# One block for the down stage and the state-space stage, a reordered first normalisation, and query and key parts stored in stacked form

## The chip, the cores and the metric

The kernel runs on one core of one Trainium2 chip. The metric is the device time of one execution in microseconds (us). A core has TensorE (PE, with its weight loads as PEld), VectorE (DVE), ScalarE (ACT), GpSimd (POOL) and SyncE (SP), which here issues every transfer; sixteen DMA engines carry the transfers out. Each engine runs its own list of instructions in order, and they meet in semaphores.

## The reference, cut to what matters

```python
x = L0_attn_x                                   # 2 batches, 512 tokens, 512 features, float32
xn = layernorm(x)
x = x + attention(xn) + ffn(xn)                 # 32 heads of 16; 512 -> 1376 -> 512
xn = layernorm(x)
x = x + state_space(xn) + lora_ffn(xn)          # in_proj 512 -> 18560, conv of 4, scan in chunks

# state_space: proj = xn @ in_proj_w.T, split into gate, xBC and dt (128 heads)
dt  = softplus(dt + dt_bias)
cum = cumsum(dt * A)                            # within a chunk
dlast, cdec = exp(cum[-1] - cum), exp(cum[-1])  # decays, per head and chunk
```

All is float32. The kernel multiplies in three products of a high and a low half (`product`: low by high, high by low, high by high), so each 512-column product of depth 512 is 12 matmuls.

## The kernel before

There are four blocks (a block ends when all engines have met): QKV with the first normalisation, attention with the gate and up products, down with the second normalisation, and the state-space stage with the output. The state-space stage takes the time from 514 us on and is touched at its beginning alone. Tokens are 8 tiles of 128 (`NTOK`); a batch is four of them.

**First normalisation** (`FirstNorm`). For each tile: DVE `moments` (L242, L244), ACT `root` (L217), DVE `scalars` (L248, L250), ACT `normalise` (L222), PE `turn` (four transposes, L210), ACT `high` (L227), DVE `low` (L255). ACT's loop does, for step t, `root(t)`, `normalise(t - 1)`, `high(t - 2)`; DVE's does `moments(t)`, `scalars(t - 1)`, `low(t - 2)`. PE does turns 0 to 4, 12 matmuls of `half(0, 0)`, turns 5 and 6, `half(1, 0)`, turn 7, and then `half(0, 1)`, which waits for the last `low`.

**QKV.** Twelve weight tiles pass through four slots (`Feed`: SP `load` L129, ACT `split_hi` L137, DVE `split_lo` L148). Tiles 0 to 7 give query and key rows: ACT `hi` (L503) and DVE `lo` (L522) make their halves, and SP's `parts(n)` stores the halves to DRAM (`qk_parts`, L427), 512 KB each. Tiles 8 to 11 are the value weights; the first value product needs all four, tile by tile. SP's order is written out: `load(n)`, then `parts(n - 6)`, and for parts 1 to 3 a `stack`, which loads the halves back with the partitions arranged as hi, hi, lo for queries and hi, lo, hi for keys (L329). Before the first `stack` SP waits until the parts of tiles 0 and 1 have landed. On ACT `split_hi(n)` stands ahead of `hi(n - 4)`. After the value product of token tile t PE does two `row_step`s (L341), the first of which waits for all eight `lo`.

**Down stage** (`emit_down`). PE adds the products of down and output projection into eight PSUM banks, one a token tile (12 matmuls each for the last four steps). DVE `add(t)` forms x and its moments, ACT takes the root, DVE `scale(t)` normalises, PE `turn_norm(t)` (L877) transposes into the same bank, ACT and DVE `low(t)` (L994) make xhi and xlo, PE `turn_sum(t)` (L883) transposes the sum into the bank again, ACT copies it and SP stores it. DVE's `low(t - 1)` comes between `add(t)` and `scale(t)`.

**Beginning of the state-space stage** (`emit_ssm`). PE multiplies the dt tile (24 matmuls into banks 2 and 3), then the entries of `ENTRIES`: B, C, g0, x0, x1, g1, x2, ... of 24 matmuls each, alternately in banks 0, 1 and 2, 3. Before entry e PE waits until entry e - 2 has been read: for B, C and x by DVE's `conv` (L1668), which needs ACT's `first_tap` (L1510). From dt come a chain of ACT and DVE work (`DT_SUM`: the cumulative sums, L1751 to L1766), then the exponentials on ACT (`DT_EXP`: L1594 and L1596), and after entries 4 and 5 PE transposes cum, dt and decays in six groups (L1468), which DVE copies out (L1773); the fifth group waits for the first copy. SP's written order around this is:

```python
            for e in range(rank(FIRST, is_tile) + AHEAD + 2):
                if e >= feed.begun:
                    weight((0, e))
                if e == 5:
                    sp.wait_ge(dt_dve, 5 + NTOK)
                    sp.dma_start(c.cum_dram[:, 0].rearrange("n h t -> h n t"), cum).then_inc(cum_out, 16)
                    sp.wait_ge(dt_act, 5 + NTOK)
                    sp.dma_start(c.cum_dram[:, 1].rearrange("n h t -> h n t"), ecum).then_inc(cum_out, 16)
                    with nc.allow_non_contiguous_dma("one value per head and chunk"):
                        sp.dma_start(c.dec_dram, ecum[:, :, CS - 1]).then_inc(cum_out, 16)
```

so weight 6 is issued behind the store of the chunk decays (`dec_dram`, called chunk_decays in the profile: 1,024 values of 4 bytes). On ACT the split of weight e + 2 of the ranked tiles, `high`, stands ahead of the tap of entry e.

Of the kernel before, what the change touches and what calls it, by code (L numbers as in the profile page):

```python
# [19 lines left out]
P = 128  # L20
# [140 lines left out]
class FirstNorm:  # L161
# [133 lines left out]
class Stacks:  # L295
# [23 lines left out]
    def stack(self, sp, c, it, i):  # L319
# [3 lines left out]
        r = it * P + i // 2 * 64  # L323
        for row, dst, side, part in ((0, self.qs, 0, 0), (1, self.qs, 0, 0), (2, self.qs, 0, 1),
                                     (0, self.ks, 1, 0), (1, self.ks, 1, 1), (2, self.ks, 1, 0)):
            for half in range(2):
                src = c.qk_rows[part, side, bass.ds(r + half * 2 * DK, 2 * DK), i % 2 * L:(i % 2 + 1) * L]
                at = half * HALF + row * DK
                sp.dma_start(dst[at:at + DK, i, :, :].bitcast(F32),  # L329
                             src.rearrange("(h d) t -> d h t", h=2)).then_inc(self.stacked[i], 16)  # L330

    def row_step(self, pe, rows, it, i, u, deep):

        n = it * NB + i
        if u == 0:
            pe.wait_ge(self.stacked[i], (it + 1) * 12 * 16)
# [57 lines left out]
def emit_qkv(nc, c, w, x_load, xhi, xlo, st, feed, tile_done, next_feed):  # L394
# [3 lines left out]
    with ExitStack() as ctx:  # L398
# [24 lines left out]
        def _(sp):  # L423
            def parts(n):
                sp.wait_ge(qk_l, n + 1)
                for part, src in enumerate((qk_hi, qk_lo)):
                    sp.dma_start(c.qk_dram[part, n % 2 * KT + n // 2], src[:, n % NR, :].bitcast(F32)  # L427
                                 ).then_inc(parts_out[n % NR], 16)
                if n == 1:
                    for s in parts_out[0:2]:  # L430
                        sp.wait_ge(s, 32)
# [16 lines left out]
            for i, s in enumerate(parts_out):  # L448
                sp.wait_ge(s, len(range(i, nqk, NR)) * 32)
# [49 lines left out]
        def _(act):  # L499
            def hi(n):  # L500
                act.wait_ge(tile_done, n + 1)
                after(act, parts_out[n % NR], n // NR * 32)
# [297 lines left out]
def emit_down(nc, c, w, xhi, xlo, hid, feed, tile_done, att_moved, oe, dt_feed, ssm_feed):  # L800

    with ExitStack() as ctx:
        sem = lambda n: ctx.enter_context(nc.semaphore(f"down_{n}"))
# [21 lines left out]
        block = ctx.enter_context(nc.Block())  # L825
# [5 lines left out]
        @block.sync  # L831
        def _(sp):
# [26 lines left out]
            for s in x_out:  # L859
                sp.wait_ge(s, NTOK // 2 * 16)  # L860

        @block.tensor
        def _(pe):
# [22 lines left out]
            for t in range(NTOK):  # L886
# [16 lines left out]
        @block.scalar  # L903
        def _(act):
# [26 lines left out]
            for t in range(NTOK + 2):  # L931
                if 1 <= t <= NTOK:
                    act.wait_ge(turned, t)
                    act.activation(xhi[:, :, tokens(t - 1)], turned_tile(t - 1), ACT.Copy).then_inc(hi_done, 1)
# [4 lines left out]
                if t >= 2:  # L939
                    act.wait_ge(x_turned, t - 1)  # L940
                    after(act, x_out[t % 2], (t - 2) // 2 * 16)
                    act.activation(xt[:, t % 2, :, :], turned_tile(t - 2), ACT.Copy).then_inc(x_copied, 1)

        @block.vector
        def _(dve):
# [58 lines left out]
        @block.gpsimd  # L1004
        def _(pool):
# [9 lines left out]


def emit_ssm(nc, c, w, xhi, xlo, feed, tile_done, dt_feed, dt_tile, semaphores, x_out):
# [14 lines left out]
    with ExitStack() as ctx:  # L1032
# [63 lines left out]
        DT_SUM, DT_EXP, DT_TURN = 1, 2, 4  # L1096
# [155 lines left out]
        def _(sp):  # L1252
# [970 lines left out]
```

## Time and profile before

| | |
|---|---|
| median of 3 runs | 2131.8 us (2131.57 to 2133.14) |
| the profiled execution, its own time | 2133.82 us |
| span of its profile | 2132.1 us, mean granted clock 0.992 |
| PE busy | 2081.6 us, 98% of the span |
| DVE, ACT, POOL busy | 69%, 63%, 41% |
| DMA | 305.34 MB, 143 GB/s on average |

Times in the profile count from the start of the span. A row of a timeline gives start and duration in us, the engine, the line, the operation with output and inputs, how many were merged, and in brackets how long the engine sat idle before it and what released it. Matmuls are pipelined, so that one of 0.39 us is followed by the next after 0.23 us; the distance of starts tells the pace.

### The profile page before, as it was taken

To read this page: it belongs to the slowest core of one execution; us is meant where nothing else is said; L and a number is where in the kernel's file an instruction comes from. 1 tells how busy PE (TensorE), PEld (TensorE's weight loads), DVE (VectorE), ACT (ScalarE), POOL (GpSimd) and SP (SyncE) were. 2 spreads that over 40 slices of the span, in tenths; PEclk is the share of its full clock that TensorE was granted. 3 is DMA by queue.
4 is the path that set the end of the run, shared out by engine and by line. 5 is a ranking of instruction groups with operands and counts; after the bars stand their busy time and mean duration, and the time that the engine had idled before them with its cause. 6 is when DMAs were issued, how large, how long until landed. Compare 5 with 4: busy or idle time off the path is not lost.

```text
span 2132.1 us, 33690 instructions
## 1 busy us (share of the span) xinstructions
PE 2081.6 (98%) x12040; PEld 1550.1 (73%) x12040; DVE 1462.3 (69%) x1811; ACT 1337.6 (63%) x2376; POOL 869.6 (41%) x762
## 2 busy tenths in 40 slices
PE   7899999998999999999999999999999999999999
PEld 5644444486777777777777777777777767888887
DVE  4466666285578778778878788687787775555555
ACT  4255555543587877888878787887878783333322
POOL 1011110130157666666757667675766682000000
PEclk9999999999999999999999999999999999999999
DMA  4422222241545555545545545555455467444452
GB/s 158 158 81 74 73 79 62 70 151 55 124 139 166 167 152 163 165 144 171 156 153 171 161 149 161 158 164 161 155 159 167 149 190 257 153 148 148 144 183 89
DMA packets 182781, 305.34 MB, mean 143 GB/s; under 512 B 20416, under 2 KB 96704, under 8 KB 182496
## 3 DMA queue, kind: packets, MB, share of 16 engines
q1 hardware_dynamic: 182624, 303.29, 45.8%
q8 instruction: 94, 1.54, 0.3%
q14 instruction: 63, 0.52, 0.1%
HBM read 249.90 MB, written 53.06 MB: 142 GB/s over the span
## 4 chain that ended last, share of the span: by engine, by line
PE 71%; ACT 2%; DVE 1%; POOL 1%; issue 1%; DMA 1%; DVEq 0%; SPq 0%; POOLq 0%; ACTq 0%
PE ssm_pp L156 16%; PE ssm_pp L158 15%; PE ssm_pp L157 15%; PE ssm_py L1444 5%; PE ssm_py L1439 4%; PE ssm_pstate L1423 4%; PE ssm_turn L1400 2%; PE ssm_py L158 1%; PE ssm_py L157 1%; PE ssm_py L156 1%; PE ssm_pp L1383 1%; PE ssm_pstate L158 1%; PE ssm_pstate L157 1%; PE ssm_pstate L156 1%; PE ssm_turn L158 1%; PE ssm_turn L157 1%
## 5 line engine op out<-in xcount | busy, mean ns | idle before, releaser
L156 PE MATMUL ssm_pp<-xhi,ssm_lo 128*128 128x512 f32 x1192 | 479.4, 402 | 4.2 <-DVE ssm_bc L1668 3.5
L158 PE MATMUL ssm_pp<-xhi,ssm_hi 128*128 128x512 f32 x1192 | 466.0, 391 | 0.0
L157 PE MATMUL ssm_pp<-xlo,ssm_hi 128*128 128x512 f32 x1192 | 465.7, 391 | 0.0
L1556 ACT ACTIVATE ssm_sct<-ssm_cumb,ssm_gpar 128x128 f32<-128x128 f32 x1024 | 313.1, 390 | 72.0 <-DMA ssm_cumb<-dt_sums 48.7
L148 POOL TENSOR_TENSOR ssm_lo<-ssm_raw,ssm_hi 128x512 fp32r<-128x512 f32 x150 | 244.1, 1633 | 92.5 <-ACT ssm_hi L137 92.5
L156 PEld LDWEIGHTS ssm_pp<-xhi,ssm_lo 128*128 128x128 f32 x1192 | 224.0, 188 | 67.5 <-issue 18.7
L1668 DVE SCALAR_TENSOR_TENSOR ssm_xc<-ssm_pp,vectors,ssm_xc 128x1022 f32<-128x1022 f32 (+2 forms) x192 | 245.2, 1277 | 36.2 <-ACT ssm_xc L1510 31.5
L158 PEld LDWEIGHTS ssm_pp<-xhi,ssm_hi 128*128 128x128 f32 x1192 | 224.2, 188 | 48.2
L157 PEld LDWEIGHTS ssm_pp<-xlo,ssm_hi 128*128 128x128 f32 x1192 | 224.3, 188 | 42.7
L1703 DVE TENSOR_TENSOR ssm_sct<-ssm_sct,ssm_cbm 128x1024 f32<-128x1024 f32 x128 | 228.4, 1785 | 27.7 <-ACT ssm_sct L1563 27.7
L1845 POOL TENSOR_TENSOR ssm_go<-ssm_t,ssm_gt 128x512 f32<-128x512 f32 x128 | 165.0, 1289 | 172.1 <-DVE ssm_t L1739 172.1
L767 ACT ACTIVATE att_pt<-att_keys 128x512 f32<-128x512 f32 x256 | 143.9, 594 | 136.0 <-PE att_keys L657 135.8
L2035 ACT ACTIVATE xlo<-ssm_gt 128x1024 fp32r<-128x1024 f32 x64 | 67.8, 1060 | 238.9 <-PE ssm_turn L158 228.1
L351 DVE TENSOR_REDUCE stk_mx<-att_rows 128x2 f32<-128x1024 f32 x112 | 137.3, 1226 | 90.5 <-PE att_rows L341 90.5
L148 POOL TENSOR_TENSOR ffn_lo<-ffn_raw,ffn_hi 128x512 fp32r<-128x512 f32 x33 | 42.9, 1301 | 375.8 <-ACT ffn_hi L137 375.8
L1715 DVE TENSOR_TENSOR ssm_xp<-ssm_turn,ssm_gpar 128x512 f32<-128x512 f32 x128 | 87.8, 686 | 151.2 <-PE ssm_turn L1400 151.2
L1444 PE MATMUL ssm_py<-ssm_sct,ssm_xp 128*64 128x128 f32 x2048 | 184.3, 274 | 0.0
L2072 DVE TENSOR_TENSOR xlo<-ssm_gt,xlo 128x1024 fp32r<-128x1024 f32 x64 | 78.4, 1225 | 149.2 <-ACT xlo L2035 149.2
L1822 POOL TENSOR_TENSOR ssm_xw<-ssm_xp,ssm_gpar 128x512 f32<-128x512 f32 x96 | 127.2, 1325 | 110.3 <-DVE ssm_xp L1715 110.2
L1439 PE MATMUL ssm_py<-ssm_cecl,ssm_state 128*64 128x128 f32 x1536 | 154.1, 279 | 0.1
L1739 DVE SCALAR_TENSOR_TENSOR ssm_t<-ssm_xc,vectors,ssm_py 128x128 f32<-128x128 f32 x512 | 142.4, 336 | 5.3 <-PE ssm_py L1444 5.3
L1444 PEld LDWEIGHTS ssm_py<-ssm_sct,ssm_xp 128*64 128x64 f32 x2048 | 124.5, 137 | 24.3 <-DVE ssm_xp L1715 18.2
(287 smaller groups left out, 4151.4 us busy)
## 6 DMA issues: line engine op xcount, KB each, us to landing
ssm_cumb<-dt_sums SPq DMA_DIRECT2D x96, 1024.0 KB, 5.9
ssm_raw<-w SPq DMA_DIRECT2D x150, 256.0 KB, 5.6
gated<-ssm_go SPq DMA_DIRECT2D x128, 256.0 KB, 4.3
ssm_cumb<-dt_sums SPq DMA_DIRECT2D x32, 512.0 KB, 4.0
ssm_gt<-w SPq DMA_DIRECT2D x64, 256.0 KB, 2.7
ssm_xc<-gated SPq DMA_DIRECT2D x32, 512.0 KB, 4.2
ssm_sct<-gated SPq DMA_DIRECT2D x32, 512.0 KB, 4.3
ffn_raw<-w SPq DMA_DIRECT2D x37, 256.0 KB, 2.8
```

Source lines behind the costliest of these rows:

```text
L148: i = dve.tensor_tensor(lo, src, hi, ALU.subtract)
L156: pe.matmul(out, wlo, xhi, start=start, stop=False)
L157: pe.matmul(out, whi, xlo, start=False, stop=False)
L158: return pe.matmul(out, whi, xhi, start=False, stop=stop)
L767: act.activation(pt[:, kt % 2, PAIRED[u % HQ], :], keys[:, u % 2, :], ACT.Exp).then_inc(exp_done, 1)
L1439: pe.matmul(p_y[r * HP:(r + 1) * HP, s % 2, ct, :], state[:, ch % 2, h * HP:(h + 1) * HP], cecl[:, s % 2, h, :], start=True, stop=False)
L1444: mm = pe.matmul(p_y[r * HP:(r + 1) * HP, s % 2, ct, :], xp[:, s % 2, h * HP:(h + 1) * HP], sct[:, s % 2, h, :], start=(ch == 0), stop=True)
L1556: i = act.activation(sct[:, s % 2, h, :], cumb[:, s % 2, 0, h, :], ACT.Relu, scale=-1.0, bias=gpar[:, unit, 0, s % NTOK, h:h + 1])
L1668: i = dve.scalar_tensor_tensor(dst[:, :, sh:L], pp[:, e % 2, :, 0:L - sh], col(conv_col(g, e) + tap), dst[:, :, sh:L], ALU.mult, ALU.add)
L1703: dve.tensor_tensor(sct[:, s % 2, :, :], sct[:, s % 2, :, :], cbm[:, s % NTOK, :].unsqueeze(1).broadcast_to([P, HU, CS]), ALU.mult).then_i ...
L1739: i = dve.scalar_tensor_tensor(t2[:, s % 2, ct, :], xc[:, s // NTOK, ct, t * CS:(t + 1) * CS], col(g * (2 * CU) + (V_D + s // NTOK * CU + ...
L1845: pool.tensor_tensor(go[:, s % 2, :, :], t2[:, s % 2, :, :], gt[:, s // NTOK, :, t * CS:(t + 1) * CS], ALU.mult).then_inc(g_done, 1)
```

## The change

1. **First normalisation:** on ACT `high(t - 2)` moves ahead of `root(t)` and `normalise(t - 1)`.
2. **Query and key parts:** DRAM now holds, for each tile, 8 heads by 3 rows (hi, hi, lo or hi, lo, hi) by 16 by tokens. `parts(n)` makes three stores of 512 KB instead of two, and `stack` makes four loads of 48 partitions instead of twelve of 16.
3. **One block:** the down stage's parts become functions of an object that the state-space block calls first, so no meeting of the engines lies between. The turns of the down stage run one tile later, and between the last turns PE does the first batch's half of the dt tile and of the B tile. B's first tap moves ahead of the logarithm on ACT, and `DT_SUM` and `DT_EXP` move one entry later, the exponentials behind the tap of x0.

```diff
     def scalar(self, act, feed):
         for t in range(NTOK + 2):
+            if t >= 2:
+                self.high(act, t - 2)
             if t < NTOK:
                 self.root(act, t)
             if 1 <= t <= NTOK:
                 self.normalise(act, t - 1)
-            if t >= 2:
-                self.high(act, t - 2)
...
-        r = it * P + i // 2 * 64
-        for row, dst, side, part in ((0, self.qs, 0, 0), (1, self.qs, 0, 0), (2, self.qs, 0, 1),
-                                     (0, self.ks, 1, 0), (1, self.ks, 1, 1), (2, self.ks, 1, 0)):
+        for side, dst in enumerate((self.qs, self.ks)):
             for half in range(2):
...
-                sp.dma_start(dst[at:at + DK, i, :, :].bitcast(F32),
-                             src.rearrange("(h d) t -> d h t", h=2)).then_inc(self.stacked[i], 16)
+                src = c.qk_heads[side, bass.ds(it * (P // DK) + (i // 2 * HQ + half * 2), 2), :,
+                                 i % 2 * L:(i % 2 + 1) * L]
+                at = half * HALF
+                sp.dma_start(dst[at:at + KSTACK, i, :, :].bitcast(F32),
+                             src.rearrange("h q t -> q h t")).then_inc(self.stacked[i], 16)
...
-                for part, src in enumerate((qk_hi, qk_lo)):
-                    sp.dma_start(c.qk_dram[part, n % 2 * KT + n // 2], src[:, n % NR, :].bitcast(F32)
+                for row, src in enumerate((qk_hi, qk_hi, qk_lo) if n % 2 == 0 else (qk_hi, qk_lo, qk_hi)):
+                    sp.dma_start(c.qk_dram[n % 2 * KT + n // 2, :, row, :, :], src[:, n % NR, :].bitcast(F32)
                                  ).then_inc(parts_out[n % NR], 16)
...
-    c.qk_dram = scratch("qk_parts", (2, 2 * KT, P, T))
-    c.qk_rows = c.qk_dram.rearrange("a (s n) p t -> a s (n p) t", s=2)
+    c.qk_dram = scratch("qk_parts", (2 * KT, P // DK, 3, DK, T))
+    c.qk_heads = c.qk_dram.rearrange("(s n) h r d t -> s (n h) (r d) t", s=2)
...
                 mm.then_inc(summed, 1)
-                if t >= 1:
-                    turn_norm(t - 1)
                 if t >= 2:
-                    turn_sum(t - 2)
+                    turn_norm(t - 2)
+                if t >= 3:
+                    turn_sum(t - 3)
+            turn_norm(NTOK - 2)
+            turn_sum(NTOK - 3)
+            dt_tile(pe, 0)
+            turn_norm(NTOK - 1)
             turn_sum(NTOK - 2)
-            turn_norm(NTOK - 1)
+            first_tile(pe, 0)
             turn_sum(NTOK - 1)
...
             for t in range(NTOK):
                 add(t)
-                if t >= 1:
-                    low(t - 1)
+                if t >= 2:
+                    low(t - 2)
                 scale(t)
+            low(NTOK - 2)
             low(NTOK - 1)
...
-        DT_SUM, DT_EXP, DT_TURN = 1, 2, 4
+        DT_SUM, DT_EXP, DT_TURN = 2, 3, 4
...
+            down.sync(sp)
             for e in range(rank(FIRST, is_tile) + AHEAD + 2):
                 if e >= feed.begun:
                     weight((0, e))
                 if e == 5:
+                    down.sums_written(sp)
                     sp.wait_ge(dt_dve, 5 + NTOK)
...
+            down.tensor(pe, dt_product, first_tile)
+            down.all_tokens(pe)
+            dt_product(pe, 1)
+            first_tile(pe, 1)
+            for e in range(1, FIRST):
...
             act.activation(dt, e_, ACT.Exp, scale=-1.0).then_inc(dt_act, 1)
+            first_tap(0, 0)
             act.wait_ge(dt_act, 3)
             act.activation(da, dt, ACT.Ln, bias=c.ones[:, 0:1]).then_inc(dt_act, 1)
             for e in range(FIRST):
-                if e == DT_EXP:
...
                     if rank(e, is_tile) + AHEAD >= feed.begun:
                         high((0, rank(e, is_tile) + AHEAD))
-                    if is_conv(e):
+                    if is_gate(e):
+                        silu(0, e)
+                    elif e > 0:
                         first_tap(0, e)
-                    else:
-                        silu(0, e)
+                    if e == DT_EXP:
+                        act.wait_ge(dt_dve, 5 + NTOK)
+                        for t in range(NTOK):
+                            act.activation(dl[:, t, :], cum[:, t, :], ACT.Exp, scale=-1.0,
+                                           bias=cum[:, t, CS - 1:CS]).then_inc(dt_act, 1)
+                        act.activation(ecum, cum, ACT.Exp).then_inc(dt_act, 1)
```

## Rows read from the trace of the kernel before

**Rows 1.** The page: busy time of each engine.

```profile
PE 2081.6 (98%) x12040; PEld 1550.1 (73%) x12040; DVE 1462.3 (69%) x1811; ACT 1337.6 (63%) x2376; POOL 869.6 (41%) x762
```

**Rows 2.** Timeline of ScalarE in the first normalisation.

```profile
7.66 0.81 ACT L222 ACTIVATE stk_v<-stk_v,ln_shift,ln_rstd 128x512 f32<-128x512 f32 x1
8.67 0.60 ACT L227 ACTIVATE xhi<-qkv_pv 128x512 fp32r<-128x512 f32 x1 [0.21 <-PE qkv_pv L210]
...
20.63 0.81 ACT L222 ACTIVATE stk_v<-stk_v,ln_shift,ln_rstd 128x512 f32<-128x512 f32 x1
...
23.86 0.81 ACT L222 ACTIVATE stk_v<-stk_v,ln_shift,ln_rstd 128x512 f32<-128x512 f32 x1
```

**Rows 3.** Timeline of TensorE in the first normalisation.

```profile
18.28 1.11 PE L210 MATMUL qkv_pv<-ident,stk_v 128*128 128x128 f32 x4 [2.10 <-ACT stk_v L222]
19.48 0.79 PE L156 MATMUL qkv_ps<-xhi,qkv_lo 128*128 128x512 f32 x1
...
24.72 0.66 PE L210 MATMUL qkv_ps<-ident,stk_v 128*128 128x128 f32 x4
...
29.96 0.50 PE L156 MATMUL qkv_ps<-xhi,qkv_lo 128*128 128x512 f32 x1 [1.41 <-DVE xlo L255]
```

**Rows 4.** Timeline of SyncE, which issues the transfers, in QKV.

```profile
36.29 0.43 SPq L427 DMA_DIRECT2D qk_parts<-qk_lo  x1
...
43.65 2.67 SPq L329 DMA_DIRECT2D stk_qs<-qk_parts  x6
...
68.29 1.01 SPq L129 DMA_DIRECT2D qkv_raw<-w  x1
...
96.19 1.55 SPq L382 DMA_DIRECT2D stk_qs<-stk_nmh  x2
```

**Rows 5.** Timeline of TensorE where QKV turns to the value product.

```profile
74.61 0.79 PE L156 MATMUL qkv_pv<-qkv_hi,xlo 128*128 128x512 f32 x1 [2.12 <-DVE qkv_lo L148]
...
76.19 1.22 PE L341 MATMUL qkv_ps<-stk_ks,stk_qs 48*128 48x512 f32 x4
...
82.20 0.73 PE L341 MATMUL qkv_ps<-stk_ks,stk_qs 48*128 48x512 f32 x4
```

**Rows 6.** Timeline of ScalarE: the last value weights' split.

```profile
73.21 0.63 ACT L137 ACTIVATE qkv_hi<-qkv_raw 128x512 fp32r<-128x512 f32 x1 [1.56 <-DMA qkv_raw<-w]
```

**Rows 7.** Windows: length, five engines' busy time, granted clock, DMA share, GB/s.

```profile
70.00:73.00 3.00, 0.98 (x3) 0.48 (x3) 1.92 (x2) 1.54 (x2) 0.00 (x0) 1.00 1.03 412
```

**Rows 8.** DMA issues of the run: count, KB each, us to landing.

```profile
qk_parts<-qk_hi SPq DMA_DIRECT2D x8, 512.0 KB, 3.9
...
stk_qs<-stk_nmh SPq DMA_DIRECT2D x32, 4.0 KB
...
chunk_decays<-ssm_xc SPq DMA_DIRECT2D x1, 4.0 KB, 10.1
```

**Rows 9.** Timeline of TensorE from the down stage's end to x0.

```profile
482.71 0.66 PE L877 MATMUL down_ps<-ident,ffn_h 128*128 128x128 f32 x4 [1.19 <-DVE ffn_h L989]
...
504.06 0.60 PE L877 MATMUL down_ps<-ident,ffn_h 128*128 128x128 f32 x4
...
514.10 0.77 PE L156 MATMUL ssm_pp<-xhi,dtw_lo 128*128 128x512 f32 x1 [3.74 <-PEq L802]
...
527.12 0.39 PE L156 MATMUL ssm_pp<-xhi,ssm_lo 128*128 128x512 f32 x1
...
542.05 0.62 PE L156 MATMUL ssm_pp<-xhi,ssm_lo 128*128 128x512 f32 x1 [3.50 <-DVE ssm_bc L1668]
```

**Rows 10.** Timeline of ScalarE: the last exponential, the split of weight 6.

```profile
540.52 1.04 ACT L1596 ACTIVATE ssm_xc<-ssm_gt 128x1024 f32<-128x1024 f32 x1
...
552.32 0.63 ACT L137 ACTIVATE ssm_hi<-ssm_raw 128x512 fp32r<-128x512 f32 x1 [1.76 <-DMA ssm_raw<-w]
```

**Rows 11.** Timeline of VectorE: a convolution and the first copies.

```profile
556.03 3.91 DVE L1668 SCALAR_TENSOR_TENSOR ssm_xc<-ssm_pp,vectors,ssm_xc 128x1022 f32<-128x1022 f32 x3 [1.53 <-ACT ssm_xc L1510]
559.86 0.87 DVE L1773 COPY ssm_gt<-ssm_py 128x128 f32<-128x128 f32 x4
```

More of the change, by code:

```diff
@@ L930, in _, with high, copy_sum @@
             ssm_feed.begin_hi(act)
[L931 to L934, printed above, removed]
+            def high(t):
+                act.wait_ge(turned, t + 1)
+                act.activation(xhi[:, :, tokens(t)], turned_tile(t), ACT.Copy).then_inc(hi_done, 1)
+            def copy_sum(t):
+                act.wait_ge(x_turned, t + 1)
+                after(act, x_out[t % 2], t // 2 * 16)
+                act.activation(xt[:, t % 2, :, :], turned_tile(t), ACT.Copy).then_inc(x_copied, 1)
+            for t in range(NTOK + 3):
+                if 2 <= t < NTOK + 2:
+                    high(t - 2)
                 if t < NTOK:
@@ L938, in _, with vector @@
                                    ).then_inc(std_done, 1)
[L939 to L945, printed above, removed]
+                if t >= 3:
+                    copy_sum(t - 3)
+        def vector(dve):
             def invert(k, half):
@@ L1014, in _, with sums_written, emit_ssm @@
             ssm_feed.begin_lo(pool)
-def emit_ssm(nc, c, w, xhi, xlo, feed, tile_done, dt_feed, dt_tile, semaphores, x_out):
+        self.sync, self.tensor, self.scalar, self.vector, self.gpsimd = sync, tensor, scalar, vector, gpsimd
+        self.first_tokens = lambda pe: pe.wait_ge(lo_done, NTOK // B)
+        self.all_tokens = lambda pe: pe.wait_ge(lo_done, NTOK)
+        self.bank_free = lambda pe, bank: pe.wait_ge(x_copied, bank + 1)
+        def sums_written(eng):
+            for q in x_out:
+                eng.wait_ge(q, NTOK // 2 * 16)
+        self.sums_written = sums_written
+def emit_ssm(nc, c, w, xhi, xlo, feed, tile_done, dt_feed, dt_tile, semaphores, down, x_out):
     with ExitStack() as ctx:
@@ L1446, in scan, with dt_product @@
                 mm.then_inc(y_done, 1)
-            pe.wait_ge(dt_feed.lo_done, 1)
-            for b in range(B):
+            def dt_product(pe, b):
+                down.bank_free(pe, B + b)
+                if b == 0:
+                    pe.wait_ge(dt_feed.lo_done, 1)
+                    down.first_tokens(pe)
                 for k in range(KT):
@@ L1453, in _, with first_tile @@
                                  xlo[:, k, b * L:(b + 1) * L], k == 0, k == KT - 1)
-            mm.then_inc(dt_tile, 1)
-            for e in range(FIRST):
+                if b == B - 1:
+                    mm.then_inc(dt_tile, 1)
+            def first_tile(pe, b):
+                down.bank_free(pe, b)
+                entry(0, 0, range(b, b + 1))
+            down.tensor(pe, dt_product, first_tile)
[3 more added lines that the diff above has]
+            for e in range(1, FIRST):
                 if e == 1:
@@ L1590, in _ @@
             for e in range(FIRST):
-                if e == DT_EXP:
-                    act.wait_ge(dt_dve, 5 + NTOK)
-                    for t in range(NTOK):
-                        act.activation(dl[:, t, :], cum[:, t, :], ACT.Exp, scale=-1.0,
-                                       bias=cum[:, t, CS - 1:CS]).then_inc(dt_act, 1)
-                    act.activation(ecum, cum, ACT.Exp).then_inc(dt_act, 1)
                 if ENTRIES[e] == "turn B":
@@ L1860, in low @@
                 feed.split_lo(pool, gg * GT, rr)
+            down.gpsimd(pool)
             for s in marks.cleared:
```

46 lines of the change are left out of this document (19 added, 27 removed).

## The prediction

> **What bounds the kernel now.** The page says that TensorE is busy 98% of the span [rows 1]. Busy time of pipelined matmuls hides their pace, so I read TensorE's timeline for the places where it stands still or runs at its lower clock, and then the other engines' timelines around those places. Everywhere else I take TensorE as the bound, and what other engines gain there is worth nothing. The change touches three such places: TensorE's starts in the first normalisation [rows 3], the two waits for value weights at 71.5 and 74.6 us, the second of 2.12 us [rows 5], and the seam from the down stage to the state-space stage, where TensorE starts the dt tile at 514.10 after 3.74 idle and waits again, 3.50, at 542.05 [rows 9]. In attention, waits for a transfer never stop TensorE, so fewer stack loads there are worth nothing: the work that hides them is the products of gate and up.
>
> **First normalisation.** No instruction is added; two pieces of ScalarE's order swap. Before, normalise(1) ran at 7.66, ahead of high(0), which could start only at 8.67, when TensorE had turned tile 0 [rows 2]. Now it stands behind high(0) and a root: 8.67 plus 0.5 plus 0.24, so about 9.4, 1.75 us late. Before, normalise(5) to normalise(6) was 3.2 us (20.63 to 23.86) [rows 2], and so were the tiles before. The new cycle is normalise 0.8, turn 1.1 [rows 3], high 0.6 and root 0.25, so 2.75. Tiles 2 to 5 then start at 12.1, 14.9, 17.6 and 20.4: tile 4's turn comes at 18.4 instead of 18.28, and the first product again at about 19.4 [rows 3]. Up to there nothing is won. After it things get worse: TensorE has 12 matmuls (19.48 to 24.18) before turn 5, high(5) waits for that turn, and normalise(6) now stands behind high(5). It starts at 24.7 plus 0.5 plus 0.25, so 25.4 instead of 23.86 [rows 2]. Turn 6, at 24.72 before [rows 3], waits until 26.3; half(1, 0) takes 2.8, turn 7, high and low 2.0 more, and the product of the second batch starts at 31.5 instead of 29.96. Cost **+1.6**; bounds 0 (if high(5) were never late) and +2.4 (if the lost time also lowers the clock for a while).
>
> **Parts and stacks.** SyncE's issue of six loads takes 2.67 us or more [rows 4]. Eight fewer loads per stack save some 3.6 us of SyncE each time, for three stacks; that is the delay which makes the last value weights late: issued at 68.29 [rows 4], split at 73.21 [rows 6], needed by TensorE at 70.2 if nothing stalled. Against it stand one more store of 512 KB per tile, which adds half to the stored bytes, and the form of all three. Before, a store's destination is 128 rows. Now it is 8 heads, each a run of 16 rows, with gaps between heads, so its outermost count is 8. If a transfer is dealt to engines along that count, 8 of 16 carry it. The nearest transfers of such a form here are the copies of negated maxima, of 8 runs: each takes SyncE 0.65 to 0.78 (1.55 for two) where a store of 128 rows takes 0.43 [rows 4], and the list of issues gives them no time to landing although it gives one for the stores [rows 8]. So something in their completion differs; they are too small to show a rate. With the engines all at work the trace shows a DMA share of 1.03 at 412 GB/s [rows 7], so the engines themselves are full, and eight of them would carry about 208 GB/s.
>
> This place the Trainium skill speaks to. "DMA: Bandwidth & Descriptors", section "Why a DMA increments its semaphore by 16 and not by 1", states that the engines used are the largest number up to 16 that divides both patterns' slowest dimension; by it the new stores would run on 8 engines and the sum would be that of eight engines below. No row here shows the rate of such a store.
>
> *With eight engines.* A store takes 524 KB / 208 = 2.5 us on the low eight, three take 7.5, and tiles come every 5.4 (24 matmuls of 0.227). A stack's loads, now of 48 rows, take all engines, 786 KB at about 310 GB/s, 2.5; a weight tile 0.65. The engines start 0.8 after the first issue, at 36.7. Parts 0, weight 7 and parts 1 end at 52.4; SyncE, which waits for them (it went on at 43.65 before [rows 4]), goes on at 53.1. The queue then holds in order stack, weight 8, parts 2, stack, weight 9, parts 3, stack, weight 10, parts 4, weight 11: three times 2.5, four times 0.65, three times 7.5, so 32.6 us, plus 0.8 until the first load moves, from 53.1: 86.5, and with landing about 87.4. Before, the split began at 73.21 [rows 6], so weights 11 come 14.2 late. Rows step 0 followed the split by 2.98 (76.19) [rows 5]; the same follows now, lower clock included. The remaining three tiles of stores end near 110, before TensorE's last row step near 118. Cost **+14.2**.
>
> *With sixteen engines.* The engines have 3.4 MB until the first wait ends (45.6) and 8.1 MB more, at 415 GB/s and 310 for stacks: weights 11 land near 67 to 69, in time. The first row steps come at 71.0, and the lower clock between 76.19 and 82.20 (6.0 us for a step that takes 3.6 at full clock) is gone: row step 1 at 74.6 instead of 82.20 [rows 5]. Gain **-7.6**.
>
> I take eight engines: of the two nearest kinds, the copies of 8 runs share the form, and the 128-row stores don't.
>
> **The seam.** Before the loop's end TensorE no longer waits for x at 482.71 (1.2, with the slow pick-up 1.35), and two turns move behind it, 0.9: the last product ends at 501.75 instead of 504.06 [rows 9]. Then come four turns, of which turn_sum(5) waits for low(5), now behind add(7), until 504.2; dt's first half 2.8 and two turns, B's first half and one turn, then dt's and B's second halves: C starts at 517.0. Before it started at 527.12 [rows 9]. So the seam itself gives 10.1. What of it survives? On VectorE and ScalarE follow z, Abs, Exp, B's tap at 517.9, B's convolution 519.05 to 522.95, C's to 527.7, the sums to 533.1; x0's product ends at 534.1, its tap at 535.3; then the table load 1.3 and the exponentials 3.4, which end at 540.0. Before they ended at 541.56 (540.52 plus 1.04) [rows 10]. Only 1.5 us is left, because the exponentials now wait for x0's tap. Behind them SyncE stores the decays, which need 10.1 us to land [rows 8], and weight 6 is queued behind: split at 552.32 before [rows 10], 550.8 now. Behind that split on ScalarE stands x1's tap, then x1's convolution 3.9 on VectorE, then the first copy 0.87 [rows 11]; TensorE's fifth group of transposes, which was at 562.07, waits for that copy: 557.2. TensorE has finished g1 at 546.6 and idles 10.5 us, loses 1.9 to the lower clock afterwards (as after 542.05, nine matmuls at 0.43 instead of 0.23), and ends x2 at 565.9 instead of 568.4. Gain **-2.6**. Bounds: -11 if the decays' store were no obstacle, 0 if weight 6 lands 2.6 later. Semaphores, buffers and the stores of x cost nothing: SyncE issues weights 3 to 5 at 512.7, before 514.06.
>
> **The sum.** +14.2 + 1.6 - 2.6 = **+13.2**. The profiled execution took 2133.82 (span 2132.1), 2.0 over the median of the runs; I put the difference on the median: 2131.8 + 13.2 = **2145.0**.
>
> **Rivals.** A measurement here can tell about 0.2%, 4.3 us, from no change.
>
> *All sixteen engines carry the stores.* The other side: -7.6 + 1.6 - 2.6 = -8.6, 2123.2, and down to 2115 with a full seam. For it: every large transfer in the trace fills all engines [rows 7]. It decides at the rate at which these stores run: at 208 GB/s they cost 14.2; the sum is zero where weights 11 land 1 us after the old time, at about 300 GB/s; above it the change wins. Chance 0.18. The Trainium skill's same page, section "Specifications", gives about 358 GB/s as a core's share of HBM; the trace shows 412 in a stretch of stores [rows 7], and by 358 this rival would gain some 3 us less.
>
> *The seam keeps its gain.* The decays' slow store doesn't hold weight 6 back, for instance because it overlaps with other traffic less than before; -11 instead of -2.6, with eight engines 2136.6. Against it: the 10.1 us stand for a transfer of 4 KB, so not its bytes but its form is slow. Chance 0.12.
>
> *Eight engines, each faster than its share.* If 412 GB/s is a limit of something shared, eight could carry 300: three stores 5.2, weights 11 at 75.8, +2.6 + 1.6 - 2.6: 2133.4. Against it: DMA share 1.03, engines full. Chance 0.08.
>
> The forecast has what is left, 0.62, with its own range 2139 to 2150 (first normalisation 0 to 2.4, issue and landing of each store +-0.2, ten of them before weights 11, +-2).
>
> **How the numbers follow.** Slower by over 0.2%: 0.62 + 0.12 + 0.02 = 0.76. Within: 0.05. Faster: 0.19. The range that leaves out 2 in 10 at most reaches from the sixteen-engine case, 2121, to 2150.
>
> **What would show it.** Right: stores of parts with a duration over 0.6 on SyncE and a DMA share near 0.5 with about 208 GB/s where only they run; last qkv split near 89 (the 1.6 included); the first row step near 92; batch two's first product at 31.5; TensorE idle for some 10 us before the fifth group of transposes. Wrong: stores at 400 GB/s, or value weights split before 75; exponentials that end more than 4 us earlier against the last down product.

## The result, and the profile after

The changed kernel takes 2152.15 us (median of 4 runs, 2151.57 to 2154.48) where the kernel before took 2132.47 in the same session: ratio 1.0090, 95% interval 1.0077 to 1.0103, **19.7 us slower**. Forecast was 13.2 us slower, 2145.0 with a range of 2139 to 2150: the direction held and the size did not. The profiled execution took 2152.64 (span 2150.9, mean granted clock 0.988).

TensorE's timeline after the change, the places that answer to [rows 3, 5, 9]:

```profile
31.71 0.50 PE L156 MATMUL qkv_ps<-xhi,qkv_lo 128*128 128x512 f32 x1 [1.41 <-DVE xlo L255]
69.73 0.76 PE L156 MATMUL qkv_ps<-xhi,qkv_lo 128*128 128x512 f32 x1 [5.08 <-DVE qk_lo L521]
89.71 0.80 PE L156 MATMUL qkv_pv<-qkv_hi,xlo 128*128 128x512 f32 x1 [8.99 <-DVE qkv_lo L148]
97.73 0.80 PE L156 MATMUL qkv_pv<-qkv_hi,xlo 128*128 128x512 f32 x1 [6.37 <-DVE qkv_lo L148]
99.31 1.22 PE L340 MATMUL qkv_ps<-stk_ks,stk_qs 48*128 48x512 f32 x4
104.47 0.73 PE L340 MATMUL qkv_ps<-stk_ks,stk_qs 48*128 48x512 f32 x4
...
546.29 0.50 PE L156 MATMUL ssm_pp<-xhi,ssm_lo 128*128 128x512 f32 x1 [0.35 <-DVE ssm_bc L1696]
579.09 1.09 PE L1494 MATMUL ssm_py<-ident,ssm_xc 128*128 128x128 f32 x4 [8.98 <-DVE ssm_gt L1802]
```

The reader is to see three things. The second batch starts at 31.71 and not at 29.96. Then TensorE stands still four times for weights or for halves that stand behind a weight's split (the three long waits are shown, the fourth is 0.92 at 79.75); the first row step comes at 99.31 and not at 76.19 [rows 5], the second at 104.47 and not at 82.20. And at the seam the wait of 3.50 for B's convolution is 0.35 now, while a new one of 8.98 stands before the fifth group of transposes.

SyncE's timeline, which answers to [rows 4]:

```profile
37.66 1.47 SPq L426 DMA_DIRECT2D qk_parts<-qk_hi  x2
39.17 2.65 SPq L426 DMA_DIRECT2D qk_parts<-qk_lo  x1
41.86 1.79 SPq L129 DMA_DIRECT2D qkv_raw<-w  x1
43.70 1.52 SPq L426 DMA_DIRECT2D qk_parts<-qk_hi  x1
45.27 1.95 SPq L426 DMA_DIRECT2D qk_parts<-qk_lo  x1
47.26 1.46 SPq L426 DMA_DIRECT2D qk_parts<-qk_hi  x1
59.70 0.81 SPq L328 DMA_DIRECT2D stk_qs<-qk_parts  x2
```

SyncE has issued its sixth store by 48.7 and goes on at 59.70; before, it went on at 43.65 [rows 4]. What the engines did in that time and after it, in windows of 4 us, columns as in [rows 7] (the last three are TensorE's granted clock, the DMA share, which is the mean busy share of the sixteen DMA engines, and GB/s):

```profile
40.00:44.00 4.00, 4.00 (x19) 3.33 (x18) 0.70 (x2) 1.01 (x2) 0.00 (x0) 1.00 0.50 124
48.00:52.00 4.00, 4.00 (x19) 3.32 (x18) 0.00 (x0) 0.00 (x0) 0.00 (x0) 1.00 0.51 179
52.00:56.00 4.00, 4.00 (x19) 3.31 (x18) 1.92 (x2) 1.55 (x2) 0.00 (x0) 1.00 0.51 211
60.00:64.00 4.00, 4.00 (x19) 3.34 (x18) 0.00 (x0) 0.00 (x0) 0.00 (x0) 1.00 0.86 170
92.00:96.00 4.00, 0.00 (x0) 0.00 (x0) 0.00 (x0) 0.00 (x0) 0.00 (x0) 0.50 0.51 206
```

Where stores fill the queue (52 to 56, 92 to 96) the share is 0.51 and the rate 206 to 211. The trace's records of single packets say the same: at most moments of these windows 8 packets are under way at once, and from 70 to 73 us in the kernel before there are 16. So half of the engines work, each as fast as before. But from 40 to 44 the stores run at 124 with the same share, and the stack's loads (60 to 64) at 170 with a share of 0.86.

ScalarE's splits of the weights behind parts and stacks; the last answers to [rows 6]:

```profile
66.79 0.63 ACT L137 ACTIVATE qkv_hi<-qkv_raw 128x512 fp32r<-128x512 f32 x1 [13.14 <-DMA qkv_raw<-w]
...
96.32 0.63 ACT L137 ACTIVATE qkv_hi<-qkv_raw 128x512 fp32r<-128x512 f32 x1 [6.48 <-DMA qkv_raw<-w]
```

A table of five places in the profiled executions (us) says where time went or came from. "Copy of B" is ScalarE's copy of B by token, behind the whole seam; from it to the end of the span it is 1550.8 before and 1550.0 after.

| | second batch | attention's first product | down's first product | copy of B | down to copy |
|---|---|---|---|---|---|
| before | 29.96 | 107.53 | 415.06 | 581.28 | 166.2 |
| changed | 31.71 | 129.75 | 438.37 | 600.89 | 162.5 |
| difference | +1.75 | +22.2 | +23.3 | +19.6 | -3.7 |

By place that is 1.75 up to the second batch, 20.5 from there to attention, 1.1 within attention (307.5 became 308.6; experiments 1 and 6, both with the old parts, show 307.3 and 308.6, so this is scatter), -3.7 at the seam, and -0.8 behind it: 18.8, the difference of the spans. These are single executions. The seam of before, unchanged in five of the experiments below (3 to 7), takes 164.6 to 165.4 there and 166.2 here; with the one block it takes 161.5 to 163.2 in three executions (the changed kernel, experiments 1 and 2). By the medians, 165.4 and 162.5, the seam gives 2.9 and not 3.7. Attention's start scatters too: four executions with the QKV block of before have it at 106.8 to 108.1.

### The profile page after: what moved, and what is told of

Its sections match the earlier page's. It is cut to its first block, busy times and chain, and to the rows that moved or that the text cites. A ratio compares the mean times of both kernels' runs of the same rounds, so it can differ in the third digit from the quotient of the medians.

```text
span 2150.9 us, 33464 instructions
## 1 busy us (share of the span) xinstructions
PE 2082.9 (97%) x12040; PEld 1551.1 (72%) x12040; DVE 1466.9 (68%) x1811; ACT 1336.5 (62%) x2376; POOL 870.4 (40%) x762
## 4 chain that ended last, share of the span: by engine, by line
PE 74%; ACT 2%; DVE 1%; POOL 1%; DMA 1%; issue 1%; SPq 0%; DVEq 0%; POOLq 0%; ACTq 0%
PE ssm_pp L156 16%; PE ssm_pp L158 15%; PE ssm_pp L157 15%; PE ssm_py L1457 5%; PE ssm_py L1452 4%; PE ssm_pstate L1436 4%; PE ssm_turn L1413 2%; PE ssm_py L156 1%; PE ssm_py L157 1%; PE ssm_py L158 1%; PE down_ps L156 1%; PE down_ps L158 1%; PE down_ps L157 1%; PE ssm_pp L1396 1%; PE ssm_pstate L158 1%; PE ssm_pstate L157 1%
```

## The experiments

Each was timed in five rounds beside the kernel before. The ratios are to it, with 95% intervals.

**1. Old parts put back.** The changed kernel with the removed lines of `stack` and `parts` (two stores, twelve loads) again.

> The changed kernel with the old parts and stacks (two stores, twelve loads) put back; the reordered first normalisation and the one block stay. Theory: the whole loss lies in the parts and stacks. The trace of the changed kernel shows its attention block 22.2 us later than before, 1.75 of it from the first normalisation, and the seam gives 3.7 back; so 2132.5 + 1.75 - 3.7 = about 2130.5, a little faster than before. Rival: the loss lies in the first normalisation or in the long block (another arrangement of memory, other waits); then this kernel stays above 2137.

2130.78, ratio 0.9990 (0.9981 to 0.9999). All of the loss was in parts and stacks. The seam, from down's first product to the copy of B, takes 163.2: 3.0 less than the 166.2 of the kernel before, 2.2 less than the median with the old seam.

**2. Three stores to 128 rows.**

```diff
-                    sp.dma_start(c.qk_dram[n % 2 * KT + n // 2, :, row, :, :], src[:, n % NR, :].bitcast(F32)
+                    sp.dma_start(c.qk_dram[n % 2 * KT + n // 2, :, row, :], src[:, n % NR, :].bitcast(F32)
...
-    c.qk_dram = scratch("qk_parts", (2 * KT, P // DK, 3, DK, T))
-    c.qk_heads = c.qk_dram.rearrange("(s n) h r d t -> s (n h) (r d) t", s=2)
+    c.qk_dram = scratch("qk_parts", (2 * KT, P, 3, T))
+    c.qk_heads = c.qk_dram.rearrange("(s n) (h d) r t -> s (n h) (d r) t", s=2, d=DK)
```

> The changed kernel with the same three stores of 512 KB and four loads a stack, but with the three rows of each partition side by side in DRAM, so that a store goes to 128 rows one behind the other and not to 8 heads of 16. Bytes and number of stores are those of the changed kernel. Theory of the form (eight engines): the DMA share passes 0.9 while stores run, and the time comes down to 2123 by the prediction's sum, or, with the stacks' loads at the 180 to 200 GB/s which the changed kernel's trace shows for them and not at 310, to about 2131. Rival, bytes: one more store a tile and more SyncE work cost what was lost; then the time stays within 3 us of 2152.

2131.65, ratio 0.9991 (0.9982 to 1.0000), 20.5 us less than the changed kernel by the medians of two sessions, with its bytes, stores and loads. Windows of this kernel, columns as above:

```profile
48.00:52.00 4.00, 4.00 (x19) 3.31 (x18) 1.91 (x2) 1.28 (x2) 0.00 (x0) 1.00 0.93 192
52.00:56.00 4.00, 4.00 (x19) 3.33 (x18) 0.83 (x2) 1.55 (x2) 0.00 (x0) 1.00 1.04 366
72.00:76.00 4.00, 0.64 (x4) 0.20 (x2) 1.65 (x2) 1.51 (x2) 0.00 (x0) 0.75 1.04 422
```

Where stores fill the queue (72 to 76) they run at 422 with a share of 1.04. The stack's loads (48 to 52) move 192 GB/s and still take 0.93 of the engines. It isn't faster than experiment 1, though: from 52 to 84 us the share is 1.02 to 1.05, where in experiment 1 it falls to 0.51 to 0.56 between stacks (56 to 60, 64 to 68). My reading is that the third store fills the time that the eight saved loads had freed.

**3. New parts alone**, in the kernel before.

> The kernel before with nothing but the new parts and stacks. If the three parts of the change add up, this shows the parts' term by itself: predicted +14.2, and by the trace of the changed kernel +20.5 (22.2 less 1.75), so 2153 and not 2146.7. Rival: the term is 14.2 and the other 6 us come from the late start that the reordered normalisation gives the transfers.

2152.86, ratio 1.0089 (1.0076 to 1.0103). Attention starts at 128.68, +21.2. The terms add up: 21.2 here against 22.2 in the changed kernel, and the late start of the normalisation isn't what made the term large.

**4. The form alone.** Two stores and twelve loads as before, with a gap behind every head (the loads read from the new places).

```diff
-                    sp.dma_start(c.qk_dram[part, n % 2 * KT + n // 2], src[:, n % NR, :].bitcast(F32)
+                    sp.dma_start(c.qk_dram[part, n % 2 * KT + n // 2, :, 0:DK, :], src[:, n % NR, :].bitcast(F32)
...
-    c.qk_dram = scratch("qk_parts", (2, 2 * KT, P, T))
+    c.qk_dram = scratch("qk_parts", (2, 2 * KT, P // DK, DK + 1, T))
```

> The kernel before, its two stores and twelve loads, with one change: in DRAM each head of 16 rows is followed by an empty row, so that a store goes to 8 runs of 16 rows. Bytes, stores and loads stay as they were. Theory of the form: stores at about half rate, DMA share near 0.5 where only they run; the wait of SyncE for the first four stores ends about 8 us later, the last value weights come some 11 us later, so 2143 (2140 to 2147). Rival, bytes: no change, 2132.5.

2150.36, ratio 1.0082 (1.0068 to 1.0096): 17.6 us, nearly the whole of experiment 3 and more than my 11. Attention starts 20.2 late, against 21.2 there: the form costs 20, and the third store with the larger loads about 1, which is within the scatter of that start. My 11 counted the stores and left out that SyncE is held up behind them. The first wait ends at 52.77, 9.1 late. The first group of six loads then takes 2.67, as before [rows 4], but the second takes 7.93 (4.14 before) and the third 7.29 (5.05 before), and from the end of that wait to the last split it takes 12.5 longer than before:

```profile
60.03 7.93 SPq L329 DMA_DIRECT2D stk_qs<-qk_parts  x6
72.56 7.29 SPq L329 DMA_DIRECT2D stk_qs<-qk_parts  x6
```

Its windows:

```profile
36.00:40.00 4.00, 4.00 (x19) 3.34 (x18) 1.92 (x2) 1.31 (x2) 0.00 (x0) 1.00 0.34 63
44.00:48.00 4.00, 4.00 (x20) 3.30 (x19) 0.00 (x1) 0.32 (x1) 0.00 (x0) 1.00 0.50 189
92.00:96.00 4.00, 0.00 (x0) 0.00 (x0) 0.51 (x1) 1.17 (x2) 0.00 (x0) 0.50 0.51 204
```

**5. Four runs instead of eight** (the same with `(2, 2 * KT, 4, 2 * DK + 1, T)` and stores to `0:2 * DK`).

> The kernel before, its two stores and twelve loads, with an empty row in DRAM behind every 32 rows, so that a store goes to 4 runs of 32 rows and not to 8 of 16. Theory that a store is dealt to as many engines as its destination has runs: 4 engines, a DMA share near 0.25 and about 103 GB/s where only stores run, a store of 512 KB takes 5.1 us; SyncE's first wait ends near 62 and the last value weights are split at 103 to 110, so 2132 + 30 to 38, 2162 to 2170. Rival: any gap in the destination halves the rate (longer runs do no harm or help a little); then 2150 or less, as with 8 runs, with a share of 0.5.

2176.69, ratio 1.0200 (1.0186 to 1.0214). SyncE goes on at 62.04 as expected; the last split is at 110.70, 0.7 past the late end of what I gave, and the time is 7 us above my range. The value products of a later tile also wait (5.27 at 143.24, for a copy of ScalarE), which my sum didn't have. The windows show the number of engines:

```profile
48.00:52.00 4.00, 4.00 (x19) 3.33 (x18) 0.00 (x0) 0.00 (x0) 0.00 (x0) 1.00 0.25 103
108.00:112.00 4.00, 0.00 (x0) 0.00 (x0) 0.64 (x1) 1.30 (x2) 0.00 (x0) 0.50 0.26 105
```

Four runs: share 0.25, 103 to 105 GB/s. Eight: 0.51, 204 to 211. 128 rows: 1.04, 422. By the packet records 4, 8 and 16 packets are under way at once, and a packet of 4,096 bytes takes 0.159 us in each of the three. Longer runs are slower, so the gap isn't the cost; the number of runs is. This is what the Trainium skill's "DMA: Bandwidth & Descriptors" says in "Why a DMA increments its semaphore by 16 and not by 1": the engines used are the largest number up to 16 that divides the slowest dimension of both patterns. The traces agree with it at 4, at 8 and at 128. They can't tell it from the plainer rule "as many engines as runs, at most 16"; a count such as 12 or 20, where the two could part, wasn't tried.

**6. The first normalisation alone.**

> The kernel before with nothing but the reordered first normalisation. Predicted +1.6; the trace of the changed kernel shows the second batch's first product 1.75 later, so 2134.3 if all of it reaches the end. Rival: the kernel with old parts and new normalisation shows that start at 31.18 and its attention block only 0.8 later than before, because the wait for the last value weight is set by transfers and takes up a part; then 2132.5 to 2133.5.

2132.92, ratio 1.0008 (0.9999 to 1.0017). The second batch starts at 30.98, +1.0, and attention at 107.66, +0.1. The rival is closer: the wait for the last value weights takes up nearly all of it, though the start of attention scatters by more than the difference. With the interval from 0 to 3.6 us the time can't tell the two.

**7. The parts in pairs**, a version that keeps the bytes of before and all sixteen engines.

```diff
-                for part, src in enumerate((qk_hi, qk_lo)):
-                    sp.dma_start(c.qk_dram[part, n % 2 * KT + n // 2], src[:, n % NR, :].bitcast(F32)
+                for row, src in enumerate((qk_hi, qk_lo) if n % 2 == 0 else (qk_lo, qk_hi)):
+                    sp.dma_start(c.qk_dram[n % 2 * KT + n // 2, :, row, :], src[:, n % NR, :].bitcast(F32)
...
+                sp.dma_start(dst[at:at + 2 * DK, i, :, :].bitcast(F32),
+                             heads.rearrange("h d r t -> (d r) h t")).then_inc(self.stacked[i], 16)
+                sp.dma_start(dst[at + 2 * DK:at + 3 * DK, i, :, :].bitcast(F32),
+                             heads[:, :, side, :].rearrange("h d t -> d h t")).then_inc(self.stacked[i], 16)
```

> The kernel before with another layout of the parts: high and low row of a partition side by side (low and high for keys), two stores a tile to 128 rows, and a stack of eight loads (four of 32 partitions, four of 16) and not twelve. Bytes as before. If SyncE's issue of loads is what makes the last value weights late (wait of 2.12 us and a lower clock behind it), this gives 3 to 6 us: 2127 to 2129. Rival: the transfers themselves, loads of stacks at 180 to 200 GB/s, set the time; then within 1.5 us of 2132.5.

2126.99, ratio 0.9978 (0.9969 to 0.9987), 4.7 us faster. Its timeline of TensorE:

```profile
73.19 0.50 PE L156 MATMUL qkv_pv<-qkv_hi,xlo 128*128 128x512 f32 x1 [2.41 <-DVE qkv_lo L148]
74.63 0.73 PE L342 MATMUL qkv_ps<-stk_ks,stk_qs 48*128 48x512 f32 x4 [0.48 <-DVE qk_lo L523]
78.28 0.73 PE L342 MATMUL qkv_ps<-stk_ks,stk_qs 48*128 48x512 f32 x4
```

A wait of 2.41 and a short one of 0.48 are left of the two, and from the first row step to the second it is 3.65 and not 6.01 [rows 5]: the granted clock is 1.00 from 72 to 80 here and falls to 0.50 there. The last split comes at 71.78, only 1.4 earlier than before, so 2.4 of the gain is the clock in this execution. The same QKV code ran once more with the lower clock (experiment 9). The time lies in the range of my theory, but the rival held in part: the last value weight is issued at 62.44, 5.9 earlier than before [rows 4], and its split gains only those 1.4, after 2.81 of waiting for the transfer. The engines were full meanwhile (from 60 to 68 us a share of 1.03 to 1.06 at 253 to 272 GB/s), so the transfers, and no longer SyncE's issue, set that time.

**8. The seam: which queue eats the gain.** Three versions of the kernel before with the one block alone and another order on SyncE. First the three stores behind weights 6 and 7:

```diff
                 if e == 5:
                     down.sums_written(sp)
+                if e == 7:
                     sp.wait_ge(dt_dve, 5 + NTOK)
                     sp.dma_start(c.cum_dram[:, 0].rearrange("n h t -> h n t"), cum).then_inc(cum_out, 16)
```

> The kernel before with the one block alone, and the three stores of sums and decays moved behind the loads of weights 6 and 7. Theory: the 10 us that the seam wins are lost again because weight 6 stands behind those stores, and x1's tap behind weight 6. With the load ahead of them x1's tap follows the exponentials at about 541.2, its convolution ends at 546.2, the first copy at 547.1 and not at 556.5; TensorE's idle time before the fifth group of transposes falls from 9 to under 2 us, and the lower clock behind it goes. So some 9 to 10 us under the one block alone: 2118 to 2121. Rival: the next wait, of another kind, takes the gain (the sums come later to the scan, or the copies wait for something else); then it stays above 2125.

2125.12, ratio 0.9967 (0.9955 to 0.9979). The first half of the theory held: the first copy ran at 545.97, TensorE's 9 us of idle time are gone. The rival held in the rest. TensorE and SyncE of this kernel:

```profile
563.94 0.79 PE L156 MATMUL ssm_pp<-xhi,ssm_lo 128*128 128x512 f32 x1 [4.66 <-DVE ssm_xc L1697]
```

```profile
549.30 0.81 SPq L1275 DMA_DIRECT2D ssm_cumb<-dt_sums  x2
550.15 1.50 SPq L129 DMA_DIRECT2D ssm_raw<-w  x2
```

Weight 8 now stood behind 2 MB of sums and was split at 558.31. Then only the decays' store moved (the line with `dec_dram` to `if e == 7`, the two stores of sums left):

> The kernel before with the one block alone, and only the store of the chunk decays (4 KB, one value a descriptor) moved behind the loads of weights 6 and 7; the two stores of sums stay ahead of them. Theory, as the prediction put it (the decays' slow store holds weight 6 back): weight 6 lands some 4 us earlier than at 550 and the kernel gains 3 to 5 us on the one block alone, about 2125. Rival, the place in the order counts and not the slow store: weight 6 is issued at 541 all the same and lands as late, 2129.

2124.86, ratio 0.9968 (0.9955 to 0.9980). Weight 6, issued at 540.41, is split at 544.41, 4.0 later; behind the decays, in experiment 1, it was issued at 541.72 and split at 550.19, 8.5 later. The rows of experiment 1 and then of this kernel:

```profile
541.08 0.59 SPq L1309 DMA_DIRECT2D chunk_decays<-ssm_xc  x1
541.72 1.83 SPq L129 DMA_DIRECT2D ssm_raw<-w  x2
550.19 0.63 ACT L137 ACTIVATE ssm_hi<-ssm_raw 128x512 fp32r<-128x512 f32 x1 [9.55 <-DMA ssm_raw<-w]
```

```profile
540.41 1.77 SPq L129 DMA_DIRECT2D ssm_raw<-w  x2
544.41 0.63 ACT L137 ACTIVATE ssm_hi<-ssm_raw 128x512 fp32r<-128x512 f32 x1 [4.45 <-DMA ssm_raw<-w]
```

So the slow store of 4 KB does hold it back, as the prediction has it, and the place in the order alone does not. TensorE still waits 4.19 before the fifth group of transposes (550.93). Then the loads of sums, too, behind weights 8 and 9 (`if e == 9`):

> The kernel before with the one block alone, the three stores behind weights 6 and 7, and the loads of the sums behind weights 8 and 9. The trace of the kernel with the stores alone moved shows TensorE's 9 us of idle time gone but a new one of 4.66 at 563.94, with the clock at half behind it: weight 8 was issued at 550.15, behind two loads of sums of 1 MB, and split at 558.31. Theory: the same queue, one step on; with weight 8 ahead of those loads this wait goes too, 4.66 and some 2 of lower clock: 2125.1 - 6 = about 2119. Rival: the sums, now later, hold up the scan at 584 or the parameters hold up something else, and it stays at 2124 or more.

2124.92, ratio 0.9961 (0.9948 to 0.9975). Not the 2119 that I expected. The wait had moved on once more, to 568.49, 4.63 long, with weight 10 issued at 562.71 behind the wait for the parameters' store. Behind it the matmuls are 0.43 apart and not 0.23 up to 574.2, about 2.6 us more, and most of that lies behind the copy of B:

```profile
568.49 0.79 PE L156 MATMUL ssm_pp<-xhi,ssm_lo 128*128 128x512 f32 x1 [4.63 <-ACT ssm_gt L1562]
```

**9. Pairs and seam together**, with the old first normalisation.

> The version that the runs point to: the kernel before with the parts in pairs (two stores, eight loads), the old first normalisation, the one block, and SyncE's order at its beginning with weights ahead of stores and of sums. If the gains add: 2132 - 4.7 (pairs) - 13 (seam) = about 2114. Rival: the two gains overlap or the seam's remaining one fails; then 2119 to 2121.

2120.11, ratio 0.9941 (0.9926 to 0.9956): the rival's time. The seam still had that last wait, and in the profiled execution the QKV block ran at the lower clock again.

**10. The last step of the queue.**

```diff
-                if e == 9:
+                if e == 10:
                     sp.wait_ge(cum_out, 48)
...
+                if e == 11:
                     sp.wait_ge(par_out, 16)
```

> The version with pairs and weights first, with two more places swapped in SyncE's order: the loads of sums stand behind weight 10, and the wait for the parameters' store with the four loads behind it stands behind weight 11. In the version before this one TensorE still waits 4.34 us at 567.15, because weight 10 stands behind the parameters (issued at 561.35, split at 565.56). Theory, one queue on SyncE all along: this wait goes too, 2120.1 - 4.3 = about 2116. Rival: the sums, issued 1 us later, or something behind them now hold up the first scan step, and the time stays at 2119 or more.

2112.34, ratio 0.9906 (0.9890 to 0.9923): **20 us faster than the kernel before, 40 faster than the changed one**, and 4 better than I expected. TensorE's only wait between 530 and 600 us:

```profile
560.42 0.50 PE L156 MATMUL ssm_pp<-xhi,ssm_lo 128*128 128x512 f32 x1 [0.24 <-ACT ssm_gt L1564]
```

From down's first product to the copy of B it takes 151.1: 166.2 before, 163.2 with the one block alone (experiment 1), 159.0, 157.9 and 155.5 in the three versions of experiment 8, 155.3 in experiment 9. In experiment 9 another 1.6 us of lower clock lie behind the copy of B, which my 2116 left out. The rest lies in the QKV block, whose code is the same in 7, 9 and 10: attention starts at 105.00 in experiment 9 and at 101.51 in 10. From the first row step to the second it took 6.57 in 9, 3.62 in 10 and 3.65 in 7. Windows of 9 and of 10:

```profile
72.00:76.00 4.00, 3.52 (x11) 2.11 (x10) 3.11 (x3) 0.60 (x1) 0.00 (x0) 0.62 0.82 336
72.00:76.00 4.00, 3.52 (x17) 2.47 (x16) 2.92 (x3) 0.60 (x1) 0.00 (x0) 1.00 0.82 314
```

Nothing in the code of 10 explains the difference, so some 3 of its 20 us may be luck, although its four runs lie within 1.2 us.

## Why the prediction was wrong in size

**First normalisation, right in its steps, too large as a cost.** The steps came as written: normalise at a distance of 2.7 (9.26, 11.94, 14.63 in the trace after), normalise(6) at 25.57 (25.4 forecast), the second batch at 31.71 (31.5), though at 31.18 and 30.98 in experiments 1 and 6. What the sum left out is that its lateness can vanish in a later wait: alone it costs attention's start 0.1 (experiment 6), where the sum has 1.6. In the changed kernel attention starts 1.1 later than in experiment 3, and the scatter of that start is as large.

**Parts and stacks, the term that was mis-sized: +14.2 forecast, 20.5 measured** (21.2 in experiment 3). The mechanism and its choice held: eight engines, decided by the form and not by the bytes (experiments 2, 4, 5). The failed step is the filling of the DMA queue, in two places.

- "A store takes 524 KB / 208 = 2.5 us": SyncE's wait was to end at 53.1, with the late normalisation 54.7, and ended at 59.70. 208 GB/s is the rate of these stores at their best, and I took it from the first packet on. Six stores and a weight are 3.4 MB and took from 39 to 59 us: 171 GB/s. That is 5.0 of the error. The packet records show two losses. From 39 to 44 us a packet takes 0.18 to 0.44 us on the mean of each microsecond, up to 1.04 for one, and 0.159 from 54 us on. And from 57 to 59 fewer than eight packets are under way at once (106 and then 69 KB in a microsecond, where eight engines carry 208), as if some engines had finished their share. Experiment 4 starts as slowly, with packets of up to 1.04 us.
- "A stack's loads at about 310 GB/s, 2.5": no run shows loads of a stack at that rate. In the kernel before 308 stands only where two stores run among them (52 to 56 us). They move 170 to 192 (the window 60 to 64, and experiment 2), 4.1 to 4.6 us a stack. Their packets hold 2,048 bytes and took 0.156 in the median (0.135 in experiment 2), nearly as long as the 4,096 of a store. That alone would be some 5 to 6 us for three stacks, but from the end of that wait to the last split it took 36.6 instead of 34.3, 2.3 more. The sum had stores and loads one after the other, and they ran partly side by side (shares of 0.72 to 0.93 from 64 to 80 us, where stores alone have 0.51). So two errors of this step partly cancelled, by luck.

Together the last split came at 96.32 and not at 89.0. From it to the first row step it took 2.99, as forecast. Of these 7.3 some 0.9 came back because the second row step lost 0.9 less to the lower clock than before.

**The rival with sixteen engines** had the same fault on the other side. Its -7.6 rested on 310 GB/s for stacks and on engines with room to spare; experiment 2 is that case, and there the term is 0.5 less than with the old parts at attention's start, or 0.9 more by the medians, nothing that can be told from zero. A part of the gain that it promised exists, 4.7 us, but it is got by fewer loads without the third store (experiment 7). The figure that the prediction cites from the Trainium skill, 358 GB/s in "Specifications" of "DMA: Bandwidth & Descriptors", didn't bind: stores reached 422.

**The seam, right in its steps.** On the scale of the kernel before (the trace of experiment 1, less its 0.6 of lateness at down's first product) the exponentials ended at 540.1 (540.0 forecast), weight 6 was split at 549.6 (550.8) and the fifth group of transposes began at 556.1 (557.2). TensorE idled 9.3 before that group there and 9.0 in the changed kernel, where 10.5 was forecast. In the changed kernel ScalarE, VectorE and SyncE show the chain as it was told:

```profile
562.29 1.05 ACT L1633 ACTIVATE ssm_xc<-ssm_gt 128x1024 f32<-128x1024 f32 x1
572.58 0.63 ACT L137 ACTIVATE ssm_hi<-ssm_raw 128x512 fp32r<-128x512 f32 x1 [9.24 <-DMA ssm_raw<-w]
```

```profile
574.24 3.91 DVE L1696 SCALAR_TENSOR_TENSOR ssm_xc<-ssm_pp,vectors,ssm_xc 128x1022 f32<-128x1022 f32 x3 [11.68 <-ACT ssm_xc L1536]
578.07 0.88 DVE L1802 COPY ssm_gt<-ssm_py 128x128 f32<-128x128 f32 x4
```

```profile
563.78 0.59 SPq L1308 DMA_DIRECT2D chunk_decays<-ssm_xc  x1
564.42 1.83 SPq L129 DMA_DIRECT2D ssm_raw<-w  x2
```

-2.6 was forecast; -3.7 in the changed kernel and -3.0 in experiment 1 came against the one trace of before, -2.9 by the medians of the traces. The rival that the seam keeps its gain was wrong for this kernel, and its price of -11 was both too high and too low: without the decays ahead of weight 6 the gain is 7 to 8, because further transfer waits stand behind the first, and with all of them gone it is 14 to 15.

**What stays open.** Why the first stores of eight runs move at about half of their later rate isn't known. Four runs start slowly too (packets of up to 0.73 us from 38 to 43). Stores of 128 rows don't start so (37 to 38 us in the kernel before: share 1.00, 406 GB/s; no packet there over 0.43 us up to 44). Why 2 KB of a stack's loads take nearly as long as 4 KB of a store isn't known either: in experiment 7 the loads' packets of the first stack took 0.084 in the median. And the traces don't say what decides whether TensorE's clock falls in the QKV block.

## What to carry to other kernels

Look at a store's destination as the transfer sees it after merging: if its outermost count is 4 or 8, that many engines carry it, and a layout with the same bytes and 128 rows one behind the other gives the rest back. A rate taken at a transfer's best is a bound, not an estimate: fill a queue with the mean of a whole stretch, loads of short rows apart from stores of long ones. And when a seam closes, follow the one in-order queue that issues the transfers for as many steps as it has entries: each wait taken away here showed the next one behind it, and only the last order paid in full.

## What the runs showed of the hardware

- A DMA share of 0.25, 0.51 and 1.04 goes with 4, 8 and 128 rows in the destination's outermost dimension, at 103, 206 and 422 GB/s.
- An issue on SyncE takes longer when much that was issued before hasn't moved yet. A store of eight runs takes 0.60 to 0.65 us with little ahead of it and 2.3 to 2.65 behind two or more others, about the 2.5 that eight engines need to move one. Six loads took 2.67 to 7.93. That a full queue is the cause is my reading.
- A DMA share near 1 doesn't mean a high rate: loads of stacks have 0.86 to 0.93 at 170 to 192 GB/s, in packets of 2 KB that take nearly as long as 4 KB of a store (0.135 to 0.156 against 0.159).
- A store of 4 KB made of single values held back the load behind it by 4.5 us (8.5 against 4.0 from issue to split), although it moves next to nothing.
- Whether TensorE's clock falls behind a short wait differed between executions of the same QKV code, and not by the length of the wait: 2.41 of idle time, then a granted clock of 1.00 (experiment 7); 1.37, then 0.50 (9); 0.81, then 1.00 (10). Each had a second wait of 0.48 behind it. The step between the row steps took 3.65, 6.57 and 3.62, so this is worth 3 us.
